# A second image group's first layers, moved from a stretch of their own into the steps of the pixel attention

## The reference, cut

```
# layer 0: attention with latents of 32 channels, then attention over 128 concepts
th, ph, g = (conv1x1(x, w) for w in (w_theta, w_phi, w_g))        # 32 x 1024
lat = softmax(th^T ph) g^T, reshaped (32, 32, 32) without a transposition
sa_out = gamma_sa * conv1x1(lat, w_o) + x
lat2 = softmax(conv1x1(sa_out, w_theta)^T concepts^T) concepts
x = gamma_moca * conv1x1(lat2, w_o) + sa_out
# layer 1: ten classes per pixel, normalised, pooled, gated
prob = conv(x) / norms;  ratio = sigmoid(relu(mean(prob) lin1^T) lin2^T)
x = gamma * einsum(prob, conv_w, ratio) + x
# layer 2: group norm, 8 heads of pixel attention (1024 x 1024), projection, residual
# layer 3: group norm, attention of the 8 heads of each pixel, projection, residual
```

## Time and profile before

| | |
|---|---|
| median of three runs | 1919.27 us (1917.6 to 1921.0) |
| the profiled execution | 1920.26 us, its span 1918.5 us |
| mean granted clock of TensorE | 0.94 of full |
| busy, share of the span: TensorE, VectorE, ScalarE, GpSimd | 89%, 72%, 41%, 71% |
| windows 0 and 1, with the first group's stages | up to about 241 us |
| first group's writes | 241 to 255 us |
| second group's stages, preparation of batch 0 | 255 to 369 us |
| windows 2 to 17 | 369 us to about 1482 us |
| layer 3 | to the end |

### The profile page before, as it was taken

The page is one execution under the profiler, slowest core; times in us unless marked ns, Lnnn a source line. Parts: engine busy times, 40 slices in busy tenths (PEclk is TensorE's granted clock), DMA queues, the critical chain, the costliest instruction groups (busy, mean ns, idle before and its releaser), DMA issues.

```text
span 1918.5 us, 37187 instructions
## 1 busy us (share of the span) xinstructions
PE 1702.5 (89%) x15160; PEld 773.6 (40%) x15160; DVE 1374.5 (72%) x2153; ACT 787.1 (41%) x1546; POOL 1357.7 (71%) x581
## 2 busy tenths in 40 slices
PE   5897765799999999999999999999997678889974
PEld 2332222344344444344344344444442345555541
DVE  5677567887777877767867877777771158878875
ACT  0352401155455555455455455455555233333320
POOL 0573600088788887887888878878789059989996
PEclk8898887799999999999999999999998889999986
DMA  5000030220001001001001010010010211222211
...
DMA packets 48432, 75.11 MB, mean 39 GB/s; under 512 B 30804, under 2 KB 31110, under 8 KB 48262
## 3 DMA queue, kind: packets, MB, share of 16 engines
...
## 4 chain that ended last, share of the span: by engine, by line
PE 77%; DVE 13%; issue 3%; ACT 2%; DMA 2%; POOL 1%; SPq 1%; POOLq 0%; DVEq 0%; ACTq 0%
PE AV L652 14%; DVE MX L1292 7%; PE S L626 6%; PE RB L895 6%; PE S L688 4%; PE S L603 3%; PE AV L908 3%; PE RB L626 3%; PE RB L944 3%; PE S L638 2%; PE RB L603 2%; PE S L630 2%; PE S L678 2%; PE RB L688 2%; PE S L634 2%
## 5 line engine op out<-in xcount | busy, mean ns | idle before, releaser
L1201 POOL TENSOR_TENSOR ACC<-ACC,PR 128x1024 f32<-128x1024 f32 x360 | 840.9, 2373 | 34.4 <-ACT PR L1034 34.4
L1034 ACT ACTIVATE PR<-S 128x512 f32<-128x512 f32 x667 | 358.6, 603 | 373.1 <-PE S L638 242.9
L1292 DVE TENSOR_REDUCE MX<-S 128x1 f32<-128x512 f32 x646 | 409.4, 681 | 124.2 <-PE RB L603 60.5
L1201 POOL TENSOR_TENSOR ACC<-PR 128x1024 f32<-128x1024 f32 x72 | 168.9, 2368 | 343.0 <-ACT PR L1034 131.6
L652 PE MATMUL AV<-PR,VT 128*32 128x512 f32 x2304 | 312.9, 616 | 3.8 <-ACT PR L1034 3.3
L1292 DVE TENSOR_REDUCE MX<-RB 128x1 f32<-128x512 f32 x336 | 218.5, 681 | 73.8 <-PE S L603 57.0
L1034 ACT ACTIVATE PR<-RB 128x512 f32<-128x512 f32 x328 | 183.7, 604 | 168.9 <-PE S L638 63.4
L626 PE MATMUL S<-HI 32*128 32x512 f32 x667 | 195.6, 493 | 6.2 <-DVE NMR L1305 2.5
L1227 POOL TENSOR_TENSOR PR<-WO,WRK 128x1792 f32<-128x1792 f32 x32 | 155.6, 4883 | 27.9 <-DMA WO<-WO 12.9
L1227 POOL TENSOR_TENSOR PR<-WO,VT 128x1792 f32<-128x1792 f32 x32 | 155.0, 4867 | 10.3 <-DMA WO<-WO 8.3
L603 PE MATMUL S<-HI 32*128 32x512 f32 x646 | 156.2, 507 | 3.4 <-ACT PR L1034 2.8
...
## 6 DMA issues: line engine op xcount, KB each, us to landing
...
WO<-WO SPq DMA_DIRECT2D x128, 16.0 KB, 1.9
```

What stands on the lines that cost most here:

```text
L1034: nc.scalar.activation(exps(s, pair)[:, HALF * one:HALF * one + HALF], RING[ring.place()], ACT.Exp, scale=1.0 if i is None else float(D) * ...
L1201: nc.gpsimd.tensor_tensor(ACC[:, pair, :], so_far, exps(s, pair), ALU.add).then_inc(pool_used, 1)
L1292: nc.vector.tensor_reduce(out=MX[:, h, t, keys:keys + 1], in_=bank(), op=ALU.max, axis=AX.X).then_inc(ring_free, 1)
```

## The change

The names of stages are the same in both kernels. What differs:

- The second group's stages from encode 1 on, and its four writes, are at the head of steps of windows 2 to 6, one each, by the table `SIDE_AT` of (window, step) pairs. Their scratch is the one of the first group (WRK), with two new buffers LATS and MIXS.
- The stretch ahead of window 2 is a list `PRELUDE`: statistics of batch 0, reread, encode, concepts and softmax of the second group, group norm, q, k, values, maxima.
- Batch 0 is read in place from X, and not stored and loaded again. Images 3, 2, 0, 1 are stored in this order; weights wait for image 3 alone, GpSimd's group norm for the store of image 2.
- The second group's store moves to SP's iteration 3 with the weights of layer 3. The output weights get a buffer of their own, loaded at the start.
- Softmax is split in softmax and scale, the reciprocal of pool in two halves (invert), and "all read" waits give way to waits for the one product needed.

```diff
+    for step, stage in side:
+        jobs[step].insert(0, stage)
...
-AFTER = [("reread", 0), ("encode", 0), ("concepts", 0), ("softmax", 0), ("encode", 1), ("turn", 0), ("mix", 0),
-         ("concepts", 1), ("softmax", 1), ("turn", 1), ("mix", 1), ("reread", 1), ("classes",), ("norms",),
-         ("pool",), ("hidden",), ("gates",), ("regate",)]
+AFTER = [("reread", 0), ("encode", 0), ("concepts", 0), ("softmax", 0), ("scale", 0), ("encode", 1), ("turn", 0),
+         ("mix", 0), ("concepts", 1), ("softmax", 1), ("scale", 1), ("turn", 1), ("mix", 1), ("reread", 1),
+         ("classes",), ("norms",), ("invert", 0), ("invert", 1), ("pool",), ("hidden",), ("gates",), ("regate",)]
 WRITES = [("write", _n) for _n in range(2 * CT)]
-AFTER_AT = (3, 3, 4, 5, 5, 6, 7, 7, 8, 9, 10, 10, 11, 12, 13, 13, 14, 15)
+AFTER_AT = (3, 3, 4, 5, 5, 5, 6, 7, 7, 8, 8, 9, 10, 10, 11, 12, 13, 13, 13, 13, 14, 15)
+BEFORE = 5
+SIDE_AT = ((2, 4), (2, 5), (2, 6), (2, 12), (2, 14), (3, 5), (3, 8), (3, 10), (3, 14), (4, 5), (4, 8), (4, 13), (5, 5),
+           (5, 8), (5, 10), (5, 13), (6, 4), (6, 5), (6, 8), (6, 10), (6, 13))
+
+
+def side_jobs(u):
+
+    return [(at[1], stage) for at, stage in zip(SIDE_AT, AFTER[BEFORE:] + WRITES) if at[0] == u]
...
-def first_jobs():
-
-
-    tiles = maxima(0)
-    jobs = {("concepts", 1): [("stats",)], ("softmax", 1): [("gn", 0)], ("turn", 1): [("gn", 1)],
-            ("reread", 1): [("qk",) + job for job in QK_ORDER[:2]],
-            ("classes",): [("qk",) + job for job in QK_ORDER[2:]],
-            ("norms",): [("v", n) for n in range(4)]}
-    for stage, n in ((("pool",), 3), (("hidden",), 2), (("gates",), 2), (("regate",), 1)):
-        jobs[stage] = tiles[:n]
-        tiles = tiles[n:]
-    jobs[("write", 0)] = [("negate", 0)]
-    jobs[("write", 1)] = [("flip", 0)]
-    return jobs
+PRELUDE = ([("stats",), ("reread", 0), ("encode", 0), ("gn", 0), ("concepts", 0), ("gn", 1), ("softmax", 0),
+            ("scale", 0)] + [("qk",) + job for job in QK_ORDER] + [("v", n) for n in range(4)]
+           + maxima(0) + [("negate", 0), ("flip", 0)])
...
-        WP_ALL = WREG2[:, 0:P_COLS + CT]
+        WP_ALL = sb("WPALL", [P, P_COLS + CT])[:, :]
...
-        WORK = [(WRK[:, 0], WRK[:, 1]),
-                (PR[:, 0:2, :].rearrange("p a n -> p (a n)"), PR[:, 2:4, :].rearrange("p a n -> p (a n)"))]
+        WORK = [(WRK[:, 0], WRK[:, 1])] * 2
         LATC = [OHU[g].rearrange("p h q -> p (h q)") for g in range(2)]
-        LAT = [VT[g].rearrange("p t c -> p (t c)") for g in range(2)]
+        LAT = [VT[0].rearrange("p t c -> p (t c)"), sb("LATS", [P, N])[:, :]]
+        MIXED = [LATC[0], sb("MIXS", [P, N])[:, :]]
...
-            for g in range(2):
-                sp.wait_ge(x_final, g + 1)
-                for b in range(H * g, H * g + H):
-                    load(out_d[b], X[:, b], x_out)
-                if g == 0:
-
-                    sp.wait_ge(x_out, 16 * H)
-                    load(XIN, out_d[0], xin_in)
-                    load(WQK_ALL, qk_pack, wqk_in)
-                    load(WV_ALL, v_pack, wv_in)
+            load(WP_ALL, p_pack, wp_in)
+            sp.wait_ge(x_final, 1)
+            load(out_d[3], X[:, 3], x3_out)
+            load(out_d[2], X[:, 2], x2_out)
+            load(out_d[0], X[:, 0], x_out)
+            load(out_d[1], X[:, 1], x_out)
+            sp.wait_ge(x3_out, 16)
+            load(WQK_ALL, qk_pack, wqk_in)
+            load(WV_ALL, v_pack, wv_in)
+            sp.wait_ge(x2_out, 16)
+            sp.wait_ge(x_out, 16 * 2)
 
             def sp_iteration(i):
-                first = i == 0
+                if i == 3:
+
+                    sp.wait_ge(x_final, 2)
+                    for b in range(H, B):
+                        load(out_d[b], X[:, b], x_out)
+                    sp.wait_ge(x_out, 16 * (2 + H))
 
                 wait(sp, xn_ready, CT * (i + 1))
                 load(XIN, out_d[(i + 1) % B], xin_in)
-                if first:
-
-                    sp.wait_ge(x_out, 16 * B)
-                    load(WP_ALL, p_pack, wp_in)
+                if i == 3:
                     load(P3_ALL, p3_pack, w3_in)
                     load(W3_ALL, w3_pack, w3_in)
                     load(B3, b3_row.broadcast_to([2, C]), masks_in)
                     load(MASKS, masks, masks_in)
-                else:
+                if i > 0:
...
-                    all_read()
...
+                    drained_at["encode"] = drained.now()
                 elif what == "concepts":
-                    all_read()
+                    wait(pe, ring_free, drained_at["encode"])
...
-            between = first_jobs()
-            for stage in AFTER + WRITES:
-                after(1, stage)
-                prepare(between.get(stage, ()))
+            prepare(PRELUDE)
...
+                    elif i is not None and s:
+                        for stage in jobs[s - 1]:
+                            after(1, stage)
...
+            pool.wait_ge(x2_out, 16)
             norm_apply(0)
...
-                wait(dve, xin_in, 16 * (batch + 1))
+                wait(dve, xin_in, 16 * batch)
...
-                            after(0, job)
+                            after(0 if i is None else 1, job)
...
+                elif what == "invert":
+
+                    cols = slice(HALF * half, HALF * half + HALF)
+                    if half == 0:
+                        dve.wait_ge(act_done, acts.add())
+                    link(nc.vector.reciprocal(NRI[g][:, cols], NRM[g][:, cols]))
                 elif what == "pool":
-
-                    dve.wait_ge(act_done, acts.add())
-                    link(nc.vector.reciprocal(NRI[g], NRM[g]))
...
+            prepare(PRELUDE[:1])
             normalise(1, 1)
-
-            between = first_jobs()
-            for stage in AFTER + WRITES:
-                after(1, stage)
-                prepare(between.get(stage, ()))
+            prepare(PRELUDE[1:])
```

39 lines of the change are left out of this document (25 added, 14 removed).

## The result

| | before | after |
|---|---|---|
| median | 1918.15 us (1916.4 to 1921.0, 5 runs) | 1929.97 us (1928.0 to 1931.8, 5 runs) |
| span of the profiled execution | 1918.5 us | 1930.0 us |
| mean granted clock of TensorE | 0.94 | 0.933 |

The change makes the kernel slower: the ratio is 1.0059, 95% interval 1.0045 to 1.0074. The prediction said 1910 us and 0.5% faster, with the rival at 1930 us as the upper end.

What follows compares the result with a forecast made beforehand. Bound by an engine-to-engine chain ahead of window 2, and by TensorE with VectorE's short gap in the windows. 1920.3 - 60.2 - 4 + 55.3 = 1911.4, less 1.0: 1910 us; own range 1903 to 1918, eight in ten 1893 to 1930.

Steps and rivals of the forecast that it cites:

- Part 1: Stretch from the first group's last write to window 2's first exponential: shortens by 60.2 us (57 to 63).
- part 3: Window 1: three "all read" waits go, saving 4 us (1 to 6).
- Part 4: Transfers: second group's stores and batch 4's reload stay hidden in window 7, 15 us to spare; no cost.
- The regimes: Ahead of window 2 an engine-to-engine chain with nothing full; in pixel attention TensorE busy 36.6 of 36.6 us per half window.
- rival A: Windows absorb vector work in VectorE's free 20%; only 38 us are paid, giving 1893 us; chance 0.17.
- part 2: Windows 2 to 6: the moved stages and four writes cost 55.3 us together (bounds 28 and 80).
- rival B: Stalls of 2 to 4 us drop TensorE's clock to 1.2 GHz; with 12 drops 1930 us, slower; chance 0.23.
- the gap: VectorE's free 0.92 us ahead of a step's first maximum, 2.1 after step 7; only vector work beyond it costs.
- the check on window 1: Stage prices tested on window 1's first half before the change: stages cost 22.2 us, 18.3 by the rule.
- Regate: Stage in windows 2 to 6, steps ahead of its readers: costs nothing.
- the scale at 3.59: Softmax scaling in the windows lasts 3.59 us beside GpSimd's additions, 2.29 where GpSimd idles; priced at 2.7.
- The estimate of 4 us: Three VectorE passes in the windows might each wait for a whole GpSimd addition, adding some 4 us; not summed.

Runs made afterwards that it cites:

- b_waits: The kernel before with only five "all read" waits of TensorE changed, three narrowed and two left out; 1909.34 us, ratio to before 0.9931.
- e_thin_adds: The changed kernel with every GpSimd addition in windows 3, 4 and 6 cut to 2 columns instead of 1024; 1923.64 us, one run.
- e_regate: The changed kernel with only regate's place moved, from step 4 to step 0 of window 6; 1933.48 us, one run.
- e_best3: e_both with the reciprocal in quarters, reread split from blend and stages re-placed, norms and gates lastly one step later; 1893.65 us, ratio to before 0.9866.
- e_both: The changed kernel with product stages behind the maxima, VectorE-only stages in steps 0 and 8, and some stages moved; 1902.98 us, ratio to before 0.9915.

## Why the prediction was wrong

**Right.** Part 1: 60.2 us forecast, 59.1 measured. That the start of GpSimd's variance came out near was luck. I had it wait for the weight pack, at 270.3, or 264.6 less the 5.7 of part 3; it started at 265.93. But the pack was issued at 253.2, 4 us after the stores, so the store that it waits for had landed by then. The variance waited for VectorE, whose operation for it (265.54) stands behind all concept scores. The first two q/k products took 3.75 and 3.12 where I had 3.75 and 2.0. Up to 3 us of it may be the narrower waits, which gave 3.3 in that stretch of b_waits, where all stages of the second group stood; no run splits them off here. Part 3: 4 forecast, 5.7 measured; I had counted three "all read" waits, and there were five. Part 4: nothing, as forecast. The regimes were read rightly too: no vector work was absorbed, rival A is out.

**Wrong: part 2**, 55.3 forecast and 77.2 measured, and with it the sign. The granted clock of 0.93 in these windows is the sign that I had named for rival B. The mechanism (a stage costs its excess over the gap) held; the size failed in two terms, which overlap in part: a stall by the lock also drops the clock.

- The clock, a term put at nothing. I wrote "My rule has none beyond what the check hides", and left the drops to rival B with 0.23. Eleven steps lost 13.8 us behind a stage, and filling the stalls took 13.4 us out of the profiled windows. With them filled, softmax and the reciprocals cost 6.1 us, where I had 6.0, against 8.7 in the changed kernel. B had 12 drops at 1.7 us, 20 us and 1930 in the end; there were 12 in this trace, of which eleven, in steps of their own, cost 1.25 us on average. My reason against it was the check on window 1, "the check came out even with such drops in it". It came out even at 22.2 us with 3.9 us unexplained, of which I took 3 for waits that the change removes. (Six products at the 1.1 us that I gave them make the base 30.0 and not 30.6, so 4.5 were unexplained.) b_waits shows these waits to be worth 5.6 us up to the last write, so the check can't be read that finely. One sum over one half window, with its own unknown of 3 us, was no ground to leave out a term of 1.7 us per stage.
- The lock. "Regate [...]: nothing", and the scale at 3.59 as in window 1. With GpSimd's additions thin the windows cost 8.4 us less; 1.3 of that were in my price of the scale. The estimate of 4 us that I gave by the Trainium skill (SBUF — State Buffer, section "SBUF: two separate sides") and did not put in the sum is what the changed kernel's operations show: the scale took 1.70 us more than alone, the blend 0.81, regate's product 2.06, together 4.6. By that rule the trace agrees, and it agrees in e_thin_adds. In e_regate the traces differ from it: the wait was more than one instruction of GpSimd, 6.3 and 5.5 us. Regate's product has only one large SBUF input, which I had not counted as such a pass.
- The writes are 15 forecast and 19.5 measured, 3.0 of it in the steps behind them. I had 3.0 for the one "where a value product stands behind"; no write was so cheap at the head of a step. At the end of a step all four are (2.7 to 3.0).

Together: 55.3, 13.4 for the clock and 7.1 for the lock are 75.8 of the 77.2, but 3.3 of the 13.4 lie in the steps of scale, reread and regate and are counted twice. Without them it is 72.5. Most of the other 4.7 are the writes, which cost 18.7 with their stalls filled. The other terms were sized well: encode, turns, mixes, concepts, classes, norms, gates and ScalarE are 27.5 forecast, and 27.4 measured without the long steps behind them.

The chances said 0.58 faster. The forecast and A had 0.67 together, and both rest on part 2 without the clock. The profile of before had the row that spoke against it; I priced it too high by a third (1.7 against 1.25 us), and gave it too small a chance. That the time came out at B's 1930 is in part luck: the clock is only some 13 us of the 22 that were missing.

**What could not be told beforehand** from the trace of before: that the place within the step is worth more than all this. The change pays 77 us for what e_best3 has for 42. Of the 35 us 28 are e_both's, products behind the maxima instead of ahead of them (22 alone) and vector work in steps 0 and 8 (14 alone); the other 7 are the quarters, the split reread, and ScalarE's places, less what differs from one execution to the next.
